# A two-layer graph and attention network on one core: the last two units' sums on VectorE, the last stage's weights loaded earlier, and the token layout by transposes

## What is computed

```python
sx = einsum('bsh,ndh->bnsd', x, hl_w) + hl_b
q = einsum('bnsd,neod->bneso', sx, wq)
k = einsum('bnsd,nod->bnso', sx, wk)
v = einsum('bnsd,nod->bnso', sx, wv)
att = softmax(einsum('bnesd,bntd->bnest', q, k) * d ** 0.5 + causal)
out = einsum('bnest,bntd->bnesd', att, v)          # zeroed where sx == 0
mixed = sum over e of out * softmax(out @ gate_w + gate_b)
f = layernorm(mixed + sx)
hx = relu(f @ fc1.T + b1); hx = layernorm(hx @ fc2.T + b2 + f)
result = hx * softmax(hx @ fgate.T)
```

## Time and profile before

| | |
|---|---|
| three runs, us | 3455.13, 3462.05, 3452.12; median 3455.13 |
| the profiled execution's own time, us | 3458.49 |
| its span, us (1.7 us lie around it) | 3456.8 |
| preparation, start to last copy of values | about 1023.5 to 1099.6 |
| attention, first PE work to last moments | about 1107 to 3310.3 |
| last stage | 3311.5 to the end |
| busy share: PE, DVE, ACT, POOL | 89%, 51%, 36%, 54% |
| granted PE clock, mean | 0.938 of full |

### The profile page before, as it was taken

How to read it: one execution, slowest core, us unless ns; L and a number is a source line. 1 busy time by engine, 2 the same in 40 slices (tenths; PEclk the granted TensorE clock), 3 DMA queues, 4 the chain that set the end, 5 groups by cost and what they waited for, 6 DMA issues and landing times. The chain is left out here.

```text
span 3456.8 us, 46110 instructions
## 1 busy us (share of the span) xinstructions
PE 3082.1 (89%) x18162; PEld 1861.7 (54%) x18162; DVE 1759.9 (51%) x2797; ACT 1237.6 (36%) x1637; POOL 1863.7 (54%) x992
## 2 busy tenths in 40 slices
PE   7999987589998889999999999689999999999943
PEld 3445656378875555555555555455555555555422
DVE  4522764487833465565555650245656564563056
ACT  2210320356531333444444444233343444444423
POOL 0000020333310356778888899446778878889924
PEclk9999888899998899999999999689999999999966
DMA  9951100399950000000000000000000000000001
GB/s 391 424 209 46 61 1 8 111 295 272 262 95 15 1 1 1 1 1 1 1 1 1 1 1 1 1 1 1 1 1 1 1 1 1 1 1 1 1 4 40
DMA packets 63748, 195.36 MB, mean 57 GB/s; under 512 B 8243, under 2 KB 25137, under 8 KB 53554
## 3 DMA queue, kind: packets, MB, share of 16 engines
q1 hardware_dynamic: 38786, 148.11, 11.1%
q0 software_dynamic: 24752, 44.31, 7.1%
HBM read 188.99 MB, written 3.41 MB: 56 GB/s over the span
## 5 line engine op out<-in xcount | busy, mean ns | idle before, releaser
L1868 POOL TENSOR_TENSOR at_acc<-at_acc,at_pt 128x1024 f32<-128x1024 f32 (+3 forms) x728 | 1557.9, 2140 | 268.3 <-ACT at_pt L1704 184.6
L1764 DVE TENSOR_REDUCE at_mx<-at_psR 128x2 f32<-128x1024 f32 (+3 forms) x784 | 860.2, 1112 | 837.9 <-PE at_psR L1595 520.0
L1704 ACT ACTIVATE at_pt<-at_psR 128x1024 f32<-128x1024 f32 (+3 forms) x784 | 731.8, 936 | 960.5 <-PE at_psR L1616 579.6
L1632 PE MATMUL at_psO<-at_pt,v 128*64 128x512 f32 (+3 forms) x3136 | 706.1, 571 | 17.0 <-DVE at_oT L1783 10.6
L1613 PE MATMUL at_psR<-at_qhi,at_klo 64*128 64x512 f32 (+3 forms) x1568 | 345.8, 436 | 38.9 <-DVE at_mx L1764 26.2
L1595 PE MATMUL at_psR<-at_khi,at_qhi 64*128 64x512 f32 (+3 forms) x1568 | 342.9, 431 | 40.0 <-ACT at_pt L1704 11.1
L1632 PEld LDWEIGHTS at_psO<-at_pt,v 128*64 128x64 f32 x3136 | 194.1, 139 | 339.7 <-issue 274.6
L1246 PE MATMUL ga_acc<-h,ga_ring 128*128 128x257 f32 (+1 forms) x1352 | 305.0, 385 | 29.5 <-ACT ga_ring L1140 26.2
L1613 PEld LDWEIGHTS at_psR<-at_qhi,at_klo 64*128 64x128 f32 x1568 | 151.9, 189 | 297.7 <-issue 273.9
L1613 PE MATMUL at_psR<-at_qlo,at_khi 64*128 64x512 f32 (+3 forms) x1568 | 299.7, 376 | 0.0
L1616 PE MATMUL at_psR<-at_nm,at_ones_r 64*128 64x512 f32 (+3 forms) x1568 | 299.1, 375 | 0.0
(11 more groups left out here) (318 smaller groups left out, 3275.8 us busy)
## 6 DMA issues: line engine op xcount, KB each, us to landing
gc_rows<-in_adj SPq DMA_DIRECT2D x26, 1664.0 KB, 17.3
ga_rows<-in_adj SPq DMA_DIRECT2D x26, 1664.0 KB, 9.9
ga_ring<-in_adjT POOLq DMA_DIRECT2D x78, 512.0 KB, 23.6
gc_cols<-in_adjT SPq DMA_DIRECT2D x26, 1024.0 KB, 14.9
gc_ring<-in_adjT SPq DMA_DIRECT2D x26, 512.0 KB, 7.5
gc_ring<-in_adjT SPq DMA_DIRECT2D x13, 256.0 KB, 2.8
ga_ring<-in_adjT POOLq DMA_DIRECT2D x13, 256.0 KB, 9.1
out_x<-X SPq DMA_DIRECT2D x6, 512.0 KB
```

The costliest lines, as they stand in the source:

```text
L1632: ins = pe.matmul(psO[lanes[l], off:off + w], v1[:, t, (2 * hp + l) * D:(2 * hp + l + 1) * D], pt[:, g % PTS, l, 0:w], start=g == FIRST[u] ...
L1704: act.activation(pt[:, g % PTS, :, 0:w], psR[:, slot_of["score", g] % SLOTS, :, 0:w], ACT.Exp).then_inc(e_ready, 1)
L1764: dve.tensor_reduce(mx[:, u % 2, :, s, c:c + 1].rearrange("p l o -> p (l o)"), psR[:, slot_of["max", i] % SLOTS, :, 0:w], AX.X, ALU.max).t ...
L1868: pool.tensor_tensor(to, to, got, ALU.add).then_inc(added, 1)
```

## The change

It has four parts.

1. **Preparation, block by block.** The second projection is gone, with its bias. Its result is the transpose of `sxT`, made on PE with the identity (two transposes per tile into `psN`) and copied by DVE into `hn`. The values are now copied by ACT instead of DVE. The three passes over all tokens become a loop over blocks: transposes of block b+1, projection of block b, then transposes and values of the tiles of block b-1. ACT's stream follows the same order.
2. **Sums of units 54 and 55 by DVE.** POOL leaves the `add_up` of these units out, and DVE does it, in the same place of the step where it had the row maxima in earlier units.
3. **Weights of the last stage.** Ten of the thirteen loads are issued by SP in the attention stage, behind its own four. `FfnWeights` holds them and their semaphore for the whole program. The other three (`back`, `fng`, `fnb`) stay in the last stage, with `back` first, under semaphores of their own. PE's `turn(0)` moves ahead of the small weight products.
4. **One buffer for `negm`**, the negated row maxima, instead of two: `maxima(u)` now waits until PE has read those of u-1 rather than of u-2.

Of the diff, the removed lines of the preparation are left out (they stand above), and so are the moved allocations.

```diff
-        for c0, w in blocks_of_tokens():
+
+    def scalar(self, eng):
+        self.scalar_root(eng)
+        self.scalar_turned(eng)
+
+    def scalar_turned(self, eng, first=0, last=NB + 1):
+        n = DC * first
+        for c0, w in blocks_of_tokens()[first:last]:
             for c in range(DC):
                 eng.wait_ge(self.turned, n + 1)
...
@@ -1284,64 +1287,90 @@
...
             @block.tensor
             def _(pe):
...
+
+                def project(b):
+                    c0, w = blocks[b]
+                    pe.wait_ge(ln.xt_ready, DC * (b + 1))
+                    for o in range(DC):
+                        n = DC * b + o
+                        if n >= 2:
+                            pe.wait_ge(x_read, n - 1)
+                        for c in range(DC):
+                            ins = pe.matmul(psX[:, n % 2, 0:w], w_sb[:, c, o * P:(o + 1) * P], xt[:, c, c0:c0 + w],
+                                            start=(c == 0), stop=(c == DC - 1))
+                        ins.then_inc(x_full, 1)
+
+                def tokens(b):
+                    c0, w = blocks[b]
+                    pe.wait_ge(x_read, DC * (b + 1))
+                    for t in range(c0 // P, (c0 + w) // P):
+                        if t >= 2:
+                            pe.wait_ge(n_read, t - 1)
+                            pe.wait_ge(v_read, t - 1)
+                        for c in range(DC):
+                            ins = pe.transpose(psN[:, t % 2, c * P:(c + 1) * P], sxT[:, c, t * P:(t + 1) * P], ident[:, :])
+                        ins.then_inc(n_full, 1)
+                        for c in range(DC):
+                            ins = pe.matmul(psV[:, t % 2, c * P:(c + 1) * P], sxT[:, c, t * P:(t + 1) * P], wv_sb[:, c, :],
+                                            start=True, stop=True)
+                        ins.then_inc(v_full, 1)
+
+                ln.tensor(pe, 0, 1)
+                pe.wait_ge(w_loaded, 48)
+                for b in range(len(blocks)):
+                    if b + 1 < len(blocks):
+                        ln.tensor(pe, b + 1, b + 2)
+                    project(b)
+                    if b:
+                        tokens(b - 1)
+                tokens(len(blocks) - 1)
 
             @block.vector
             def _(dve):
                 ln.vector(dve, Linker(dve, chain))
...
+                    dve.wait_ge(ln.turned, DC * (t // SUB + 1))
+                    dve.tensor_copy(hn[:, t, :], psN[:, t % 2, 0:DM]).then_inc(n_read, 1)
 
...
+                ln.scalar_root(act)
+
+                def project(b):
+                    c0, w = blocks[b]
+                    for o in range(DC):
+                        n = DC * b + o
+                        act.wait_ge(x_full, n + 1)
+                        act.activation(sxT[:, o, c0:c0 + w], psX[:, n % 2, 0:w], ACT.Identity,
+                                       bias=bT_sb[:, o:o + 1]).then_inc(x_read, 1)
+
+                def tokens(b):
+                    c0, w = blocks[b]
+                    for t in range(c0 // P, (c0 + w) // P):
+                        act.wait_ge(v_full, t + 1)
+                        act.activation(v1[:, t, :], psV[:, t % 2, 0:DM], ACT.Copy).then_inc(v_read, 1)
+
+                ln.scalar_turned(act, 0, 1)
+                act.wait_ge(w_loaded, 48)
+                for b in range(len(blocks)):
+                    if b + 1 < len(blocks):
+                        ln.scalar_turned(act, b + 1, b + 2)
+                    project(b)
+                    if b:
+                        tokens(b - 1)
+                tokens(len(blocks) - 1)
...
+LAST_POOL = NU - 2
...
+                ffn.load(sp, io)
...
                     c0, bw = QBLOCKS[UNITS[u][1]]
                     dve.wait_ge(p1_read, CHUNKS_UPTO[u + 1])
-                    if u >= 2:
-                        dve.wait_ge(x_full, turn_of["r", u - 2] + 1)
+                    if u >= 1:
+                        dve.wait_ge(x_full, turn_of["r", u - 1] + 1)
                     for s in range(bw // P):
                         seen = (c0 // P + s) // SUB + 1
-                        ins = dve.tensor_reduce(negm[:, u % 2, s, 0:D + 1:D], mx[:, u % 2, :, s, 0:seen], AX.X, ALU.max, negate=True)
+                        ins = dve.tensor_reduce(negm[:, s, 0:D + 1:D], mx[:, u % 2, :, s, 0:seen], AX.X, ALU.max, negate=True)
...
+                def add_up(g):
+                    u, t, off, w = GROUPS[g]
+                    dve.wait_ge(e_ready, g + 1)
+                    dve.wait_ge(added, g)
+                    to, got = acc[:, u % 2, :, off:off + w], pt[:, g % PTS, :, 0:w]
+                    if t == 0:
+                        dve.wait_ge(x_full, last_turn(u - 2) + 1)
+                        dve.tensor_copy(to, got).then_inc(added, 1)
+                    else:
+                        dve.tensor_tensor(to, to, got, ALU.add).then_inc(added, 1)
...
@@ -1846,6 +1888,9 @@
                             turn(*x)
                         for x in gate_pieces(u, k):
                             gate(*x)
+                        if u >= LAST_POOL:
+                            add_up(FIRST[u] + 2 * k)
+                            add_up(FIRST[u] + 2 * k + 1)
...
@@ -1892,32 +1937,51 @@
                                        fill=NEG, base=0, pattern=[[-D, 2], [1, P]], channel_multiplier=-1).then_inc(hides, 1)
                 for u in range(NU):
                     for k in range(steps_of(u)):
-                        add_up(FIRST[u] + 2 * k)
-                        add_up(FIRST[u] + 2 * k + 1)
+                        if u < LAST_POOL:
+                            add_up(FIRST[u] + 2 * k)
+                            add_up(FIRST[u] + 2 * k + 1)
                         for x in gate_pieces(u, k):
                             gate(*x)
                 gate(NPR - 1, NQB - 1, 1)
 
 
...
+        self.loaded = m.sem("ff_w_loaded")
+
+    def load(self, sp, io):
+        for dst, src in ((self.fc1[:, :], io["fc1"]), (self.fc2[:, :], io["fc2"]), (self.b1[:, :], io["fc1_b"]),
+                         (self.b2[:, :], io["fc2_b"]), (self.lng[:, :], io["ln_g"]), (self.lnb[:, :], io["ln_b"]),
+                         (self.fngT[:, :], io["fnorm_gT"]), (self.fnbT[:, :], io["fnorm_bT"]),
+                         (self.fgw[:, :, :], io["fgate"].rearrange("(c p) n -> p c n", p=P)),
+                         (self.fgw2[:, :, :], io["fgate2"].rearrange("c p n -> p c n"))):
+            sp.dma_start(dst, src).then_inc(self.loaded, 16)
+
...
+                sp.dma_start(back[:, :, 0:P], io["centering"].rearrange("c p n -> p c n")).then_inc(back_loaded, 16)
+                sp.dma_start(fng[:, :], row_on_all(io["fnorm_g"])).then_inc(norm_loaded, 16)
+                sp.dma_start(fnb[:, :], row_on_all(io["fnorm_b"])).then_inc(norm_loaded, 16)
...
@@ -2027,13 +2086,14 @@
                                             start=True, stop=True)
                     ins.then_inc(back_full, 1)
 
+                turn(0)
                 pe.wait_ge(prep_v, 2)
+                pe.wait_ge(back_loaded, 16)
                 for c in range(DC):
                     pe.matmul(psF[:, 0, c * GW:(c + 1) * GW], back[:, c, 0:P], fgw2[:, c, :], start=True, stop=True)
                 for c in range(DC):
                     ins = pe.matmul(psF[:, 1, 0:NH], fnb_all[:, :], fgw[:, c, :], start=(c == 0), stop=(c == DC - 1))
                 ins.then_inc(prep_t, 1)
-                turn(0)
                 pe.wait_ge(prep_s, 1)
...
-                pool.wait_ge(w_loaded, 13 * 16)
+                pool.wait_ge(norm_loaded, 32)
...
+        ffn = FfnWeights(m)
```

105 lines of the change are left out of this document (30 added, 75 removed).

## The result

| | before | after |
|---|---|---|
| median of the runs, us | 3456.2 (3452.1 to 3462.1, 4 runs) | 3408.8 (3406.7 to 3411.0, 4 runs) |
| the profiled execution's own time / span, us | 3458.5 / 3456.8 | 3406.7 / 3405.0 |
| granted PE clock, mean | 0.938 | 0.941 |

A forecast was written before the change was run, and what follows sets the result against it. Each place on its own: PE bound the preparation, POOL's adds the last two units, a weight load the last stage's start. 3458.5 - 19.0 - 17.3 - 5.8 + 1.0 = 3417.4, less 3.4: 3414 us, range 3406 to 3427.

The forecast's parts named there:

- Preparation: Preparation stage: PE bounds it, and transposes replacing the second projection end it at 1080.2 instead of 1099.1 us, -19.0.
- The start at half clock: Start of the preparation: PE runs at its lower clock level for some 5.5 us and loses 2.7 us.
- the forecast's sign: Preparation: PE's work would last 53 us from its first transpose, not 72.
- The best case, -20: Preparation: the bound on the gain if PE had no waits at all, -20 us.
- Units 54 and 55: Last two attention units: with DVE adding, PE sets the pace, -14.7, and the turning out keeps full clock, -2.6; together -17.3.
- Last stage: Start of the last stage: nothing waits for weights, first layer 10.7 us in instead of 16.45, -5.8.
- The new clear: Program end: clearing the weights' longer-lived semaphore, with a barrier, costs +1.0 us, between 0 and 1.2.
- A: Preparation: the copies by DVE and ACT pace the tokens, 3430 us in full, 3422 at half; chance 0.15.
- B: Preparation: PE stays at its lower clock, by the transpose rule or short waits, +26, 3459 us; chance 0.04.
- C: Units 54 and 55: DVE's sums collide with POOL, 2.92 us per add giving 3459, 3.60 giving 3495; chance 0.02.
- D: Units 54 and 55: POOL held PE up only by the final lag, gain 8.5 instead of 17.3, 3423; chance 0.07.
- E: Attention's start: the clock rises earlier after the different preparation, worth up to 10 us more, 3404; chance 0.07.

The follow-up runs named there:

- x_sums: The kernel before with only the sums of exponentials of units 54 and 55 moved from POOL to DVE; 3444.4 us, ratio 0.9951.
- x_again: The changed kernel measured once more, as it is; 3414.5 us, ratio 0.9869 to the kernel before.
- x_four: The changed kernel with DVE doing the sums of the last four units instead of two; 3423.7 us, ratio 0.9898 to the kernel before.
- x_first: The changed kernel with the last stage's small products ahead of the transposes of block 0; 3410.9 us, ratio 0.9859 to the kernel before.
- x_early: The changed kernel with the attention's four loads and POOL's constants moved into the preparation; 3403.6 us, ratio 0.9839 to the kernel before.
- x_warm: The changed kernel plus 24 unused products after the last turning out and 8 at the last stage's start; 3412.3 us, ratio 0.9867 to the kernel before.
- x_best: The changed kernel with the moves of x_early and x_first together; 3403.8 us, ratio 0.9835 to the kernel before.
- x_loads: The kernel before with only the early last-stage loads, turn(0) first and the single negm; 3451.9 us, ratio 0.9984.
- x_coll: The changed kernel with an unused POOL addition beside each group of units 54 and 55; 3480.4 us, ratio 1.0059 to the kernel before.
- x_fill: x_best with unused products in PE's waits at the attention's start, after the last turning out and in the last stage; 3388.6 us, ratio 0.9784 to the kernel before.

## Why the prediction was right, step by step

**Preparation: -19.0 forecast, -23.7 measured** (-23.1 alone). The mechanism was right, three terms were too large. *"Eight transposes take 1.04 us at full clock, 0.13 each"*: the row's last 0.16 us overlap the next instruction; the pace is 0.11, and 104 of them make 11.4 us, not 13.6. *"104 records at 0.97 / 8, 12.6 us"*: also 0.11, 11.4. *"I allow 1.6 for waits"*: there are hardly any. The start at half clock cost what was said. PE's work lasts 48.6 us from its first transpose, where the forecast's sign was 53. The best case, -20, was built from the same durations and so was no bound. The 21.8 us of the pass that goes are read off a row that the edge of its view had cut short: from start to start it is 22.5 (1060.82 to 1083.30). No term uses it.

**Units 54 and 55: -17.3 forecast, -18.8 measured** (12.4 and 6.4 in the table; x_sums -18.6). PE sets the pace at 3.91 us a step, DVE's add takes 1.22, as forecast. *"A whole unit is then 53.7 us"* is right from the first exponential of unit 54 to that of unit 55, 53.3 in the trace, and too long for unit 55, which has no unit behind it. From `take_out` to `take_out` unit 54 took 52.49 us and unit 55 took 49.75. In unit 54 PE also turns the row maxima of unit 55 (its second step takes 4.49 us, that of unit 55 takes 3.92), and it makes the first scores of unit 55 ahead of the last products with the values; unit 55 has neither. The start of the turning out moved by 17.4, not 14.7. *"So it should still run at full clock"* was half right: the first half did, the second ran at 0.82 and 0.85 per group. Instead of 2.6 it gained 1.3. Which it is changes from kernel to kernel with the same work there: in six of the others (x_again, x_four, x_first, x_early, x_warm, x_best) the second half ran at full clock too.

**Last stage: -5.8 forecast, -7.2 measured** (x_loads -5.95). First layer at 10.7 us forecast, 10.33 measured, 6.1 earlier than before. The remaining 1.1 are not a gain that repeats: the last stage as before took 136.7, 135.5 and 135.4 us in three executions, and with the new start, in the same order, 127.7 to 130.8 in seven. The new clear: +1.0 forecast, +0.15 measured. The loads, forecast at nothing: +0.35, inside the bound of 2.

**Rivals.** A fell: no PE group has a wait, so the copies don't pace it. B fell, for the clock was at 1.00 for 41 us with transposes through all of it. Products stand among them there; the stretch in which PE does nothing but transposes is that of the earlier trace rows, where the clock rises from 0.50 to 0.94. By the rule that the Trainium skill gives (page "TensorE: Matmul & The Clock Gate", Part 4: PE-mode transpose) it would not rise; these rows contradict it. C's mechanism was shown by x_coll: 3.30 from one full sum to the next, where 1.22 and 2.38 make 3.60. The lock that the Trainium skill describes (page "SBUF — State Buffer", Who interferes with whom) is such an alternation; the run agrees but for these 0.3 us. D fell by x_sums. E did not happen by itself (0.54 in the attention's first 35 us, 0.55 before), but the reserve that it named exists, and x_fill took it.

**The total.** The terms sum to -41.1 against the execution before; the traces show -49.5 in the same places. Another 2.3 lie before the preparation and in the attention up to unit 53, which makes the 51.8 of the spans. Subtracting the 3.4 us by which that execution lay above its median was right in sign: with the fourth run it is 2.2 above, the execution after is 2.1 under its own median, and so the medians are 47.5 apart. The attention alone moves by up to 11 us among kernels with the same work there. The range, 3406 to 3427, held both measurements, 3408.8 and 3414.5, but by its lower end, and that was partly luck: two of the three gains, 23.7 and 18.8, passed the best cases of 20 and 18.5, and all three terms erred to the same side.

## What to carry to other kernels

Price a run of equal PE instructions by the distance between starts, not by the duration of a row, whose end overlaps the next instruction (0.88 against 1.04 us for eight transposes). When one engine's tail is moved to another, move only what that engine's own queue leaves room for, and not beside instructions of an engine that it must take turns with, as in x_coll. And before tuning an edge of a few microseconds, read the granted clock behind it: a short wait of PE at a stage's start can cost more by what it does to the clock than by its own length.

## What the runs showed of the hardware that I had not expected

Eleven products without use, in waits that were there anyway, changed the granted clock from 0.54 to 0.97 over 35 us and made unit 0 end 6.8 us earlier. In x_warm the first layer's product, behind a wait of 1.59 us, took 3.65 us instead of 1.98, although the clock had been at 1.00 from 10 us before the stage until the product began. The same stretch of the attention, with the same 13522 records of PE, took 2068.8 to 2079.7 us, and the longest has the lower mean clock (0.95 against 0.96). What decides when the clock rises there stays open: the traces show that it differs, not why. And a POOL instruction of 4.54 us with all its operands in SBUF made two DVE sums take 5.78 us in place of 2.55.
